# Loading the edge features of the second layer in blocks of 128 KB, not in quads of 512 KB

## The reference

```python
h = jnp.maximum(_layernorm(x, axis=-1), 0.0)
# second layer: weight=h, review_feat=edge_attr_64 (206250 x 64), attn=edge_weight
pa = jax.nn.sigmoid(review_feat @ prob_w.T)
ra = jax.nn.sigmoid(review_feat @ review_score_w.T)
rf = review_feat @ review_w.T
h_src = weight[src_idx]
cj_e = cj[src_idx]
m = (h_src * pa + rf * (ra * a)) * cj_e
h = jax.ops.segment_sum(m, dst_idx, num_segments=ci.shape[0])
x = x + h * ci
```

## Time and profile before

| | us |
|---|---|
| median of 3 runs | 6132.26 |
| lowest and highest run | 6117.36, 6136.0 |
| the profiled execution | 6118.99 |
| its span, first to last instruction | 6116.3 |
| DVE busy | 4662.3 (76%) |
| PE busy | 4418.4 (72%) |
| POOL busy | 3568.6 (58%) |
| ACT busy | 2592.6 (42%) |

### The profile page before, as it was taken

The page is one execution under the profiler, slowest core; times in us unless marked ns, Lnnn a source line. Parts: engine busy times, 40 slices in busy tenths (PEclk is TensorE's granted clock), DMA queues, the critical chain, the costliest instruction groups (busy, mean ns, idle before and its releaser), DMA issues.

```text
span 6116.3 us, 108132 instructions
## 1 busy us (share of the span) xinstructions
PE 4418.4 (72%) x25058; PEld 2776.0 (45%) x25058; DVE 4662.3 (76%) x10241; ACT 2592.6 (42%) x6354; POOL 3568.6 (58%) x3639
## 2 busy tenths in 40 slices
PE   5799999999999999999999933344444444444444
PEld 4555555555555555555555513333333333333333
DVE  3488888888888888888888866667766676676675
ACT  3677776767776767767677640000000000000000
POOL 0255655555556556556555536566666666666665
PEclk9999999999999999999999965555555555555555
DMA  8533333333333333333333342222222222222221
GB/s 215 190 75 77 76 77 75 78 75 77 76 75 78 74 77 77 75 76 76 77 75 77 74 123 44 44 46 45 47 47 46 46 46 50 45 46 45 49 46 34
DMA packets 324279, 435.66 MB, mean 71 GB/s; under 512 B 132852, under 2 KB 204756, under 8 KB 323068
## 3 DMA queue, kind: packets, MB, share of 16 engines
q0 software_dynamic: 122512, 173.81, 16.4%
q1 hardware_dynamic: 188284, 250.00, 13.9%
q10 hardware_dynamic: 13296, 9.92, 0.9%
HBM read 362.45 MB, written 70.96 MB: 71 GB/s over the span
## 4 chain that ended last, share of the span: by engine, by line
PE 38%; DVE 32%; issue 12%; another core or an unknown queue 12%; ACT 3%; DMA 1%; DVEq 1%; ACTq 0%; POOL 0%; SPq 0%; POOLq 0%
PE ps_beta L1937 11%; PE ps_hidden L1885 8%; PE ps_hidden L1886 6%; DVE dots L1761 4%; DVE work L1333 4%; PE ps_beta L1945 3%; PE ps_sum L1956 3%; DVE table_sb L1640 3%; DVE work L1755 3%; DVE centered L1640 3%; DVE work L1794 2%; DVE work L1800 2%; PE ps_alpha L1919 2%; DVE equal L1787 2%
## 5 line engine op out<-in xcount | busy, mean ns | idle before, releaser
L786 POOL DMA_INDIRECT ends<-split_table,parts x1612 | 1581.0, 981 | 1532.9 <-issue 1399.2
L1885 PE MATMUL ps_hidden<-ends_parts,w_high 128*128 128x512 f32 x2418 | 1094.9, 453 | 114.4 <-DVE work L1333 65.7
L839 POOL DMA_INDIRECT work<-src_table,parts x808 | 805.5, 997 | 601.0 <-DVE work L1800 308.4
L1333 DVE TENSOR_TENSOR work<-work,ps_hidden 128x512 f32<-128x512 f32 x1612 | 1102.7, 684 | 15.2 <-ACT work L923 2.4
L923 ACT ACTIVATE work<-ps_hidden 128x512 f32<-128x512 f32 x1612 | 955.7, 601 | 143.8 <-PE ps_hidden L1886 102.5
L839 POOL DMA_INDIRECT ends<-src_table,parts x804 | 813.0, 1011 | 313.4 <-issue 240.6
L1886 PE MATMUL ps_hidden<-ends_hot,window 128*128 128x512 f32 x2418 | 955.5, 395 | 0.0
L2143 PE MATMUL ps_beta<-work,equal 128*128 128x128 f32 x1616 | 413.9, 437 | 729.2 <-DVE work L1800 577.6
L1338 DVE TENSOR_TENSOR beta<-beta_scaled,ps_beta 128x512 f32<-128x512 f32 x806 | 552.2, 685 | 412.4 <-ACT beta_scaled L981 349.8
L1126 ACT ACTIVATE ps_alpha<-dots 128x8 f32<-128x8 f32 x403 | 72.0, 179 | 1841.8 <-DVE dots L1761 1156.8
L1937 PE MATMUL ps_beta<-work,msg_w_sb 128*64 128x512 f32 x3224 | 825.0, 611 | 3.9 <-DVE work L1333 0.2
(11 more groups left out here) (220 smaller groups left out, 6713.5 us busy)
## 6 DMA issues: line engine op xcount, KB each, us to landing
window<-window_table SPq DMA_DIRECT2D x403, 192.5 KB
parts<-in_edge_attr SPq DMA_DIRECT2D x101, 512.0 KB
dst_rows_sb<-in_dst_rows SPq DMA_DIRECT2D x403, 128.0 KB
ends<-split_table,parts POOLq DMA_INDIRECT x1612
window_table<-parts SPq DMA_DIRECT2D x49, 386.0 KB
sums<-key_rows POOLq DMA_DIRECT2D x403, 32.6 KB
work<-src_table,parts POOLq DMA_INDIRECT x808
ends<-src_table,parts POOLq DMA_INDIRECT x804
```

The costliest lines, as they stand in the source:

```text
L786: pool.indirect_dma_start(out=ends[m][:, t, :], out_offset=None, in_=split_table, in_offset=bass.IndirectOffsetOnAxis(ap=src_all[:, b * T ...
L839: pool.indirect_dma_start(out=ends1_windows[m][:, t, :], out_offset=None, in_=src_table, in_offset=bass.IndirectOffsetOnAxis(ap=src_all[:, ...
L1333: nc.vector.tensor_tensor(hidden[k][:, :], scaled[k % NL][:, :], ps_hidden[k % NL][:, :], ALU.max).then_inc(hidden_ready, 1)
L1885: nc.tensor.matmul(o, w1_high[:, k * P:(k + 1) * P], ends_parts[j][:, :], start=True, stop=False)
```

## The change

One DMA of 512 KB per quad becomes four of 128 KB, one for each block. The wait ahead of each is now on the block: the piece for block `m` of quad `q + 3` is issued when block `m - 1` of quad `q` has been finished, and the piece for `m == 0` when quad `q - 1` has, as before. Storing rows and loading the window of `x`, which came once per quad after the feature load, now come after the piece for `m == 1`. Each of the four pieces raises `feat_in[k]` by 16, and DVE waits for 64 per quad, where it waited for 16. The four buffers, the bytes and their places are the same. The loads ahead of the loop are split in the same way.

```diff
-            def load_feat(quad):
+            def load_feat(quad, m):
                 k = quad % 4
-                sp.dma_start(feat_quads[k].rearrange("p b t d -> p b (t d)"),
-                             edge_attr[bass.ds(4 * quad, 4)].rearrange("b p t d -> p b (t d)")).then_inc(feat_in[k], 16)
+                sp.dma_start(feat_quads[k][:, m, :, :], edge_attr[4 * quad + m]).then_inc(feat_in[k], 16)
...
-            for quad in range(2):
-                load_feat(quad)
+            for b in range(8):
+                load_feat(b // 4, b % 4)
             sp.wait_ge(sums0_landed, 1)
             for c in range(NCH):
                 read_sums0(c)
-            load_feat(2)
+            for m in range(4):
+                load_feat(2, m)
...
-            load_feat(3)
+            for m in range(4):
+                load_feat(3, m)
             for quad in range(NQ):
-                if quad >= 1 and quad + 3 < NQ:
-                    sp.wait_ge(terms1_step, 16 * quad)
-                    load_feat(quad + 3)
-                if quad >= 2:
-                    send_rows(quad - 2)
-                load_x_window(quad)
+                for m in range(4):
+                    if quad >= 1 and quad + 3 < NQ:
+                        sp.wait_ge(terms1_step, 16 * quad + 4 * m)
+                        load_feat(quad + 3, m)
+                    if m == 1:
+                        if quad >= 2:
+                            send_rows(quad - 2)
+                        load_x_window(quad)
...
                 if m == 0:
-                    dve.wait_ge(feat_in[quad % 4], 16 * (quad // 4 + 1))
+                    dve.wait_ge(feat_in[quad % 4], 64 * (quad // 4 + 1))
```

## The result

| | us |
|---|---|
| before, median of 12 runs | 6130.84 (6116.77 to 6137.55) |
| after, median of 12 runs | 6147.47 (6137.78 to 6157.79) |
| ratio after/before, 95% interval | 1.0026 [1.0018, 1.0034] |
| the profiled execution of after | 6157.79, span 6156.2 |

The changed kernel is slower by some 16 us (16.6 by the medians), a quarter of a per cent, and the interval leaves out 1. The forecast was 99 us faster. The result lies nearest to the rival "nothing changes" (6132).

The account below looks back on a forecast made before the run. The prediction took waits in the second layer, mainly DVE's at L1770 for PE's late signals, as the bound. All terms were 0 but 99 us gained: 6119 - 99 = 6020, plus 13 for the median, 6033 us; range 5880 to 6200.

Parts of the forecast that it names:

- nothing changes: Rival, chance 0.25: in the second layer PE's signals are late because POOL's gathers run without a break; 6132 us.
- What bounds the kernel: Second layer: waits, not engines or bandwidth; 379.1 us ahead of L1770 for PE's late signals, at most some 381 us gainable.
- More DMAs on SP: Three more DMAs per quad on SP's queue, 1.2 us, hidden by its waits for DVE; taken as 0.
- waits on SP: SP's store of rows and window of `x`, now behind a new wait, still come early enough; 0.
- later features: A quad's last piece is issued three blocks later, still about nine blocks before its first reader; 0.
- between the layers: Six more issues ahead of the sums, three ahead of the tables; taken as 0, at most 1.3 us.
- The landing in one burst: At L1770, a landing of 0.6 instead of 2.4 us shortens each of 55 waits by 1.8 us: 99 us gained.
- The gathers: POOL's gathers held up by landings: between 34 us gained and 102 us lost; taken as 0.
- The burst sets it off: Rival, chance 0.15: 528 packets at once start a backlog; without it L1770's waits go and POOL bounds, 5752 us.
- Slower: Rival, chance 0.28: any landing sets off late signals, now at four places per quad; 79 us more, 6211 us.

Follow-up runs that it names:

- experiment 7: L1770 moved to the quad's last block: in the kernel before, ratio 0.9994 (signals on time); in the changed kernel, 0.9941 (late) and 0.995 (on time).
- r_before: The kernel before, unchanged, traced on another chip where signals are on time: 5647.94 us, one execution.
- Experiment 1: The kernel before without feature loads in the second layer's loop: ratio 0.9946 with signals on time, 0.9997 with signals late.
- experiment 2: The kernel before with fewer gathers per second-layer block than four: one, 5213.62 us (signals on time); two, 5350.64 us (late chip).
- e1_again: The kernel before without feature loads in the second layer's loop, on a chip with late signals: 6126.93 us, ratio 0.9997.
- e2b_two_gathers: The kernel before with two gathers per second-layer block, not four, from block 4 on, on the late chip: 5350.64 us, one execution.
- e1_no_load: The kernel before without feature loads in the second layer's loop, on a chip with signals on time: 5612.24 us, ratio 0.9946.

## Why the prediction was wrong

**What bounds the kernel** was read rightly for the chip of the profile: waits, the greatest of them ahead of L1770 for a signal of PE, and POOL's idle time as their other side. Too narrow was that it is PE's signals that arrive late, since DVE's own do so too (experiment 7). The prediction took L1797, with 48.7 us, for a wait for the gathers; it is one of these, and the wait for the gathers stands ahead of L1794. That POOL is the bound once DVE isn't late came out as well: on on-time chips DVE waits for gathers for some 408 us. The price named for DVE's lateness, 381 us, was near too: in `r_before` the gathers run from 3503.0 to 5632.5 us, which is 2129.5 us and 340 less than the 2469 of the earlier trace rows. (The two profiled spans are 468 us apart; nearly all of the rest is the first layer, after which the gathers start some 124 us sooner there.)

**More DMAs on SP, waits on SP, later features, between the layers:** each was put at 0. L1758 without idle time bears out the features. On on-time chips the others cost little too, as eight pieces lose little against four. On the chip of the result something costs 16 us, and it may be one of these; which, stays open.

**The landing in one burst** is the step that failed. It was given 99 us, and no run shows any of it: with the burst cut to a blip L1773 waits for 410.6 us, and without any landing L1767 waits for 374.5 us. The fault was in the sentence "I take 99 us, since both rows are then true: a wait with a burst and a wait without one." That a wait also occurs without a burst made the burst needless as a cause. A term for it should have had a row of its own that asked for it, such as a longer wait where a burst was near, and there was none: 8.54 us without and 8.33 us with one are equal. The link rested on place alone, and place had an innocent cause: a feature load comes once per quad, and L1770 comes once per quad, at a fixed distance.

**The gathers** were put at 0 between a gain of 34 and a loss of 102 us. The bound of 34 us was the good value where the gathers are the bound: 26.7 us shorter in sum, 29 us in time. On the chip of the result the gathers got shorter by 7.9 us, and the 57.6 us more for which POOL waited for DVE outweigh that. The Trainium skill, DMA: Bandwidth & Descriptors, section Bandwidth, with its advice to batch DMAs to 1 MiB or more, spoke against the change. By the runs, splitting 512 KB into four spread over the blocks is 29 us faster on an on-time chip, and four back to back are equal to one. The measurement decides; 16 us lost on the chip of the result may or may not be of the kind that the section means. (The 2.0 us and the 436 GB/s of the prediction stand in that page's section Anatomy of one DMA, for DMAs issued from GpSimd; the loads here are issued from SP.)

**Rivals.** "Nothing changes" had the better half of the mechanism: signals are late because of POOL's gathers. Experiment 1 bears out that the landings have no part, experiment 2 that the gathers have one. Its other half, that signals recover when the gathers stop, isn't borne out. Here is one wait in the trace of before that ends while the gathers run on:

```profile
4076.12 0.94 POOL L839 DMA_INDIRECT work<-src_table,parts  x1 [0.30 <-issue]
4077.37 0.95 POOL L839 DMA_INDIRECT work<-src_table,parts  x1 [0.30 <-issue]
4077.53 0.28 DVE L1770 SCALAR_TENSOR_TENSOR parts<-ps_hidden,ci_windows,parts 128x64 f32<-128x64 f32 x1 [3.92 <-remote]
...
4078.62 1.21 POOL L839 DMA_INDIRECT work<-src_table,parts  x1 [0.30 <-issue]
```

After 24 of the 55 waits of L1770 the next gather comes at the same distance of 0.30 us, with no pause. The longest wait of all, 15.34 us, goes on for 3.5 us after the last gather is over:

```profile
5982.71 0.95 POOL L839 DMA_INDIRECT work<-src_table,parts  x1 [0.30 <-issue]
5987.19 0.28 DVE L1770 SCALAR_TENSOR_TENSOR parts<-ps_hidden,ci_windows,parts 128x64 f32<-128x64 f32 x1 [15.34 <-remote]
```

How the gathers delay a signal, and what lets it through, stays open. "The burst sets it off" falls by `e1_again`. "Slower" had the sign but not the cause: the four places in each quad caught one more instance of L1773 (56 for 55), not eleven, and in place of its 79 us the wait grew by 31.5. What the prediction didn't think of is that the lateness might depend on the chip, or its state, and not on the kernel alone.

## What to carry to other kernels

Before two things that fall at one place are tied together, find the row where one of them occurs alone; if it looks the same there, the other gets 0 in the sum. Where signals come late in themselves, moving one wait may hand most of the time to the next (here 362 us came off one line and 34 out of the time), unless what makes them late goes. Before a late signal is put down to the engine that raised it, look at a wait of an engine for its own signal: if that is late too, the engine isn't the cause. An edit may have one sign on one chip and the other on the next, because another engine is the bound there: run it on more than one before it is kept.

## What the runs showed of the hardware

- A semaphore signal from PE may arrive some 10 us after the matmul that raises it: L2167 over at 5047.83, L1770 released at 5057.79; in after 4988.14 and 5000.91. DVE waited for its own signal for 7.70 and 5.17 us (experiment 7). With two gathers of POOL per block, not four, this all but went away on a chip that had it (`e2b_two_gathers`, one execution: 3.5 us ahead of L1797 is what is left of such waits of DVE).
- The same program took about 6130 us on one chip and in the runs of the result, and 5640 on four others, 8% apart, each with a spread of well under 1%. Where it took 5640, its trace shows no late signals (`r_before`, L1770: 2 waits, 6.8 us). The first layer differs as well. These are 1000 us of it for the kernel before and for `r_before` (stretch, length, busy PE, PEld, DVE, ACT, POOL, PEclk, DMA, GB/s):

```profile
1000.00:2000.00 1000.00, 969.51 (x6061) 534.39 (x6059) 867.44 (x1702) 706.81 (x1612) 585.12 (x605) 1.00 0.34 76
```

```profile
1000.00:2000.00 1000.00, 984.39 (x6288) 560.60 (x6287) 899.05 (x1765) 730.78 (x1674) 610.01 (x628) 1.00 0.37 79
```

  The granted clock is 1.00 in both, and yet 6288 matmuls get done for 6061. DVE raises `terms1_step` 1612 times; the trace of `r_before` holds 1611 rises and that of before 907. Whether signals then arrive several at once or records are missing isn't told. What makes the difference stays open.
- An indirect gather of 128 rows takes POOL 0.94 us in the median (`r_before`: 0.945) and up to 2.49 us. One that lay across small DMAs of SP took 1.60 us, but gathers of over 1.4 us are found in `e1_no_load` too, 38 of 1458.
